# The routing stage of a two-layer kernel: one VectorE operation for the gated sum, variances by fours, tiles of coefficients on three engines, another order of TensorE's work

## What is computed

```python
# after the first layer: x (8, 128, 512), z = (x - mean) * rsqrt(var + eps) along the features
# gate: per batch and feature, one of two values, chosen by a 0/1 choice `top` of each token
x3 = x + coef * z                      # coef = top * dA + other, two numbers per batch and feature
# routed experts, on the normalised x3
xn = (x3 - mean(x3)) * rsqrt(var(x3) + eps)
logits = xn @ router_w.T + router_b    # 8 experts
top2 -> softmax over the two best, zero elsewhere
h = xn @ A.T                           # 8 experts x rank 16 = 128
out = x3 + (8 / R) * (h * gate) @ Bm
```

## Time and profile before

| | |
|---|---|
| median of 3 runs | 1065.99 us (1065.75 to 1067.38) |
| the profiled execution's own time | 1069.71 us |
| its span, first to last instruction | 1068.0 us |
| TensorE busy | 93% of the span |
| VectorE, ScalarE, GpSimd busy | 65%, 48%, 44% |
| mean granted TensorE clock | 0.973 of full speed |

### The profile page before, as it was taken

The page is one execution under the profiler, slowest core; times in us unless marked ns, Lnnn a source line. Parts: engine busy times, 40 slices in busy tenths (PEclk is TensorE's granted clock), DMA queues, the critical chain, the costliest instruction groups (busy, mean ns, idle before and its releaser), DMA issues.

```text
span 1068.0 us, 18238 instructions
## 1 busy us (share of the span) xinstructions
PE 996.8 (93%) x6004; PEld 843.0 (79%) x6004; DVE 697.6 (65%) x1827; ACT 512.6 (48%) x1328; POOL 467.5 (44%) x366
## 2 busy tenths in 40 slices
PE   5999999999999999999999999999999999869376
PEld 4888888888888888888888888888888888734263
DVE  5567565666577767677564575566567557678755
ACT  4454444444444445445543544445355354345561
POOL 4555444444444555443354344346435334226241
PEclk9999999999999999999999999999999999969768
DMA  6422222223333332333322222213222221000002
GB/s 219 161 92 87 95 95 89 91 95 96 96 97 98 98 97 83 104 112 98 106 84 84 85 67 72 83 42 98 73 74 84 80 69 53 23 21 1 0 2 79
DMA packets 50412, 87.71 MB, mean 82 GB/s; under 512 B 6368, under 2 KB 15200, under 8 KB 50336
## 3 DMA queue, kind: packets, MB, share of 16 engines
q1 hardware_dynamic: 50336, 86.76, 25.4%
HBM read 84.64 MB, written 2.10 MB: 81 GB/s over the span
## 4 chain that ended last, share of the span: by engine, by line
PE 79%; DVE 7%; issue 6%; POOL 3%; DVEq 2%; ACT 2%; DMA 1%; SPq 0%; POOLq 0%; ACTq 0%
PE pX L1731 15%; PE pX L1733 14%; PE pX L1732 14%; PE pT L1983 5%; PE oacc L1731 5%; PE oacc L1732 5%; PE oacc L1733 5%; PE pS L1915 5%; PE pS L1736 2%; PE pA L2043 1%; POOL wv_lo L570 1%; PE pX L1848 1%; PE pX L1904 1%; PE pT L1904 1%; PE pX L1736 1%
## 5 line engine op out<-in xcount | busy, mean ns | idle before, releaser
L570 POOL TENSOR_TENSOR wq_lo<-raw_q,wq_hi 128x512 fp32r<-128x512 f32 x64 | 82.6, 1290 | 264.2 <-DVE prob L1376 257.9
L1731 PE MATMUL pX<-wv_lo,cT_hi 128*128 128x256 f32 x512 | 149.5, 292 | 0.2 <-ACT q_sb L740 0.2
L1359 DVE TENSOR_TENSOR score<-pS,b_mask 128x512 f32<-128x512 f32 x64 | 44.2, 691 | 156.8 <-PE pS L1915 144.7
L868 ACT ACTIVATE prob<-score,neg_max 128x128 f32<-128x128 f32 x256 | 99.8, 391 | 97.4 <-DVE neg_max L1362 97.4
L1732 PE MATMUL pX<-wv_hi,cT_lo 128*128 128x256 f32 x512 | 144.3, 282 | 0.0
L1733 PE MATMUL pX<-wv_hi,cT_hi 128*128 128x256 f32 x512 | 144.2, 282 | 0.0
L570 POOL TENSOR_TENSOR wv_lo<-raw_v,wv_hi 128x1024 fp32r<-128x1024 f32 x32 | 77.1, 2409 | 121.9 <-ACT wv_hi L740 121.9
L740 ACT ACTIVATE v_sb<-pX 128x512 f32<-128x512 f32 x64 | 38.2, 597 | 163.6 <-PE pX L1733 163.6
L1731 PE MATMUL pX<-xT_lo,wq_hi 128*128 128x512 f32 x252 | 104.4, 414 | 5.7 <-POOL wq_lo L570 5.0
L1731 PE MATMUL oacc<-wo_lo,aT_hi 128*128 128x512 f32 x256 | 101.8, 398 | 3.5 <-DVE aT_lo L1351 2.3
L1731 PE MATMUL pX<-cT_lo,wk_hi 128*128 128x512 f32 x252 | 103.0, 409 | 0.0
(11 more groups left out here) (308 smaller groups left out, 2377.4 us busy)
## 6 DMA issues: line engine op xcount, KB each, us to landing
raw_k<-in_wk SPq DMA_DIRECT2D x64, 256.0 KB, 2.8
raw_q<-in_wq SPq DMA_DIRECT2D x64, 256.0 KB, 3.5
raw_v<-in_wv SPq DMA_DIRECT2D x32, 512.0 KB, 3.9
raw_o<-in_wo SPq DMA_DIRECT2D x64, 256.0 KB, 2.6
b_raw<-in_bias SPq DMA_DIRECT2D x64, 64.0 KB, 2.5
g_raw<-in_w_gate SPq DMA_DIRECT2D x16, 172.0 KB
g_raw<-in_w_up SPq DMA_DIRECT2D x16, 172.0 KB
f_raw<-in_w_down SPq DMA_DIRECT2D x4, 688.0 KB, 4.1
```

The lines of the kernel that those rows point to most:

```text
L570: g.tensor_tensor(w_lo[c][:], w_raw[c][:], w_hi[c][:].bitcast(F32), ALU.subtract).then_inc(s_w_lo[c], 1)
L868: e = a.activation(prob[:, b, :], score[:, b, :], ACT.Exp, bias=neg_max[:, b:b + 1], accum_out=row_sum[:, b:b + 1])
L1359: v.tensor_tensor(score[:], pS[:].rearrange("p (b s) -> p b s", b=HB), b_mask[:], ALU.add).then_inc(s_scored, 1)
L1731: mm(dst, lh, rl, start=start, stop=False, skip_group_check=lint)
```

## The change

In `gated`, VectorE now adds sigma = 1/rstd of z (two reciprocals, ahead of the stage) to the bank and multiplies by z, straight into `xr`: coef z + x = (coef + sigma) z + mean. The mean is left out of `xr` until the last step; GpSimd's addition and the tile `zc` fall away here. The statistics are one `bn_stats` for each batch, with the rest for four batches together and one power for four. `rh` is copied without a scale; the scale enters the logits (one operation for each batch) and, with 8/R, the gates. The four coefficient tiles of a batch go two to ScalarE, one to VectorE, one to GpSimd (batch 0: one and three to ScalarE and VectorE). The table load stands behind ScalarE's first five tiles. TensorE's order is routed_transposes(t + 1), router(t), coef_transposes(t + 3), and the experts' products all come after the last router. The results of batches 0 to 3 go through SBUF: ScalarE adds the mean (`lora_out`), then VectorE adds batches 0 and 1 and GpSimd 2 and 3 to `xr`, all after VectorE's second `weighed`. SP waits accordingly. The diff, without declarations, the VectorE helpers that only move and the old lists already told in words:

```diff
             for t in range(B):
-                sp.wait_ge(s_x4_done, t + 1)
+                if t in (2, 3):
+                    sp.wait_ge(s_x4_pool, t - 1)
+                else:
+                    sp.wait_ge(s_x4_done, t + 1 if t < 2 else t - 1)
                 sp.dma_start(out[t], xr[:, t, :]).then_inc(s_out[t % 2], 16)
...
-            for t in range(B):
-                pool.wait_ge(s_zc, t + 1)
-                g.tensor_tensor(xr[:, t, :], zc[:, t % 2, :], xr[:, t, :], ALU.add).then_inc(s_x3, 1)
-                if t >= 1:
-                    routed_rstd(t - 1)
-            routed_rstd(B - 1)
+            def one_coef(t):
+                g.tensor_scalar(coef[:, t, KT - 1, :], top[:, t // HB, KT - 1, t % HB, :], dA[:, KT - 1, t:t + 1],
+                                other[:, KT - 1, t:t + 1], ALU.mult, ALU.add).then_inc(s_coef_pool, 1)
+
+            def routed_rstd(i):
+                pool.wait_ge(s_x3_var, i + 1)
+                g.tensor_tensor(rs3[:, i * HB:(i + 1) * HB], ve3[:, i * HB:(i + 1) * HB], neg_half[:, 0:HB],
+                                ALU.pow).then_inc(s_x3_rstd, 1)
+
+            pool.wait_ge(s_coef_dve, 1)
+            one_coef(1)
+            one_coef(2)
+            for t in range(3, B):
+                pool.wait_ge(s_x3, t - 2)
+                one_coef(t)
+            routed_rstd(0)
+            routed_rstd(1)
+            for t in (2, 3):
+                pool.wait_ge(s_lora_sb, t + 1)
+                pool.wait_ge(s_x4_done, 2)
+                g.tensor_tensor(xr[:, t, :], lora_sb[t], xr[:, t, :], ALU.add).then_inc(s_x4_pool, 1)
...
             def routed_heads(t):
                 act.wait_ge(s_r_proj, t + 1)
-                act.wait_ge(s_x3_rstd, t + 1)
-                a.activation(rh[:, t, :], pA[:, 0:E + ER], ACT.Copy,
-                             scale=rs3[:, t:t + 1]).then_inc(s_rh, 1)
+                copy(rh[:, t, :], pA[:, 0:E + ER]).then_inc(s_rh, 1)
...
+            def lora_out(t):
+                act.wait_ge(s_l_proj, t + 1)
+                a.activation(lora_sb[t], l_bank[t % 2], ACT.Identity, bias=e_zmv[:, t, 0:1]).then_inc(s_lora_sb, 1)
+
+            weights_of(0, (3,))
+            weights_of(1, (0, 1))
+            weights_of(2, (0, 1))
+            a.activation(exp_again[:], ident[:, 0:1], ACT.Exp)
+            routed_out(0)
+            weights_of(3, (0, 1))
+            for t in range(HB):
+                routed_out(t + 1)
+                routed_heads(t)
+                weights_of(t + 4, (0, 1))
+            routed_out(5)
+            routed_heads(4)
+            routed_out(6)
+            routed_heads(5)
+            route_exp(0)
+            routed_out(7)
+            routed_heads(6)
+            routed_heads(7)
+            lora_in(0)
+            lora_in(1)
+            lora_out(0)
+            lora_in(2)
+            lora_out(1)
+            lora_in(3)
+            route_exp(1)
+            lora_out(2)
+            lora_out(3)
             for t in range(HB, B):
-                lora_out(t)
+                lora_in(t)
...
             def gated(t):
                 dve.wait_ge(s_c_trans, t + 1)
-                if t >= 2:
-                    dve.wait_ge(s_x3, t - 1)
-                v.tensor_tensor(zc[:, t % 2, :], c_bank[t % 2][:], z[:, t, :], ALU.mult).then_inc(s_zc, 1)
+                v.scalar_tensor_tensor(out=xr[:, t, :], in0=c_bank[t % 2][:], scalar=sigma[:, t:t + 1],
+                                       in1=z[:, t, :], op0=ALU.add, op1=ALU.mult).then_inc(s_x3, 1)
...
+            weights_of(0, (0, 1, 2))
+            weights_of(1, (2,))
+            weights_of(2, (2,))
             dve.wait_ge(s_e_z_again, HB)
             dve.wait_ge(s_z_act, 2)
             gated(0)
             gated(1)
+            for t in range(HB + 1):
+                if t + 3 < B:
+                    weights_of(t + 3, (2,))
+                dve.drain()
+                routed_stats(t)
+                if t == HB - 1:
+                    variances_of(0)
+                if t + 2 < 7:
+                    gated(t + 2)
+            routed_stats(5)
+            top_logits(0)
+            gated(7)
+            routed_stats(6)
+            chosen(0)
+            routed_stats(7)
+            variances_of(1)
+            gates(0)
+            for t in range(HB):
+                weighed(t)
+            top_logits(1)
+            chosen(1)
+            gates(1)
+            for t in range(HB, B):
+                weighed(t)
+            lora_sum(0)
+            lora_sum(1)
             for t in range(HB, B):
                 finished(t)
...
             def lora(t):
                 pe.wait_ge(s_hwT, t + 1)
-                if t >= 2:
-                    pe.wait_ge(s_x4_done, t - 1)
+                if 2 <= t < HB + 2:
+                    pe.wait_ge(s_lora_sb, t - 1)
+                elif t >= HB + 2:
+                    pe.wait_ge(s_x4_done, t - HB + 1)
...
             coef_transposes(0)
             coef_transposes(1)
+            routed_transposes(0)
+            coef_transposes(2)
+            for t in range(B - 1):
+                routed_transposes(t + 1)
+                if t == 0:
+                    pe.wait_ge(s_ra, 1)
+                router(t)
+                if t + 3 < B:
+                    coef_transposes(t + 3)
+            router(B - 1)
+            hidden_transpose(0)
             for t in range(HB):
+                lora(t)
+                hidden_transpose(t + 1)
             hidden_transpose(5)
             for t in range(HB, B):
                 lora(t)
                 if t + 2 < B:
                     hidden_transpose(t + 2)
```

More of the change, by code:

```diff
@@ L245, in layers_kernel @@
         post.close()
+        lora_sb = [t[:, i].rearrange("p k s -> p (k s)") for t in (e_split, e_junk) for i in range(2)]
         sum_junk = zc[:].rearrange("p i (k s) -> p i k s", k=KT)
@@ L298, in layers_kernel @@
         s_coef = sem("coef")
-        s_coef_first = sem("coef_first")
+        s_coef_dve = sem("coef_by_dve")
+        s_coef_pool = sem("coef_by_pool")
+        s_lora_sb = sem("lora_sb")
         s_const_in = sem("const_in")
@@ L1049, in _, with weights_of @@
             last.then_inc(s_sig, 1)
-            a.activation(exp_again[:], ident[:, 0:1], ACT.Exp)
             act.wait_ge(s_dA, 1)
-            def weights_of(t):
-                for lt in range(KT):
+            def weights_of(t, parts):
+                for lt in parts:
                     last = a.activation(coef[:, t, lt, :], top[:, t // HB, lt, t % HB, :], ACT.Identity,
@@ L1075, in route_exp, with lora_in @@
                              ACT.Exp).then_inc(s_r_exp, 1)
-            def lora_out(t):
+            def lora_in(t):
                 act.wait_ge(s_hw_t, t + 1)
@@ L1637, in _, with weights_of @@
             dve.drain()
-            for lt in range(KT):
-                last = v.tensor_scalar(coef[:, 0, lt, :], top[:, 0, lt, 0, :], dA[:, lt, 0:1], other[:, lt, 0:1],
-                                       ALU.mult, ALU.add)
-            last.then_inc(s_coef_first, 1)
-            dve.wait_ge(s_e_z_again, HB)
-            dve.wait_ge(s_z_act, 2)
+            def weights_of(t, parts):
+                for lt in parts:
+                    last = v.tensor_scalar(coef[:, t, lt, :], top[:, t // HB, lt, t % HB, :], dA[:, lt, t:t + 1],
+                                           other[:, lt, t:t + 1], ALU.mult, ALU.add)
+                last.then_inc(s_coef_dve, 1)
@@ L1652, in routed_stats, with variances_of @@
             def routed_stats(t):
-                dve.wait_ge(s_x3, t + 1)
                 v.bn_stats(st3[:, t, :], xr[:, t, :])
+            def variances_of(i):
                 dve.drain()
-                v.bn_aggr(mv3[:, t, :], st3[:, t, :])
+                for t in range(i * HB, (i + 1) * HB):
+                    v.bn_aggr(mv3[:, t, :], st3[:, t, :])
                 dve.drain()
-                v.tensor_scalar(ve3[:, t:t + 1], mv3[:, t, 1:2], EPS, None, ALU.add).then_inc(s_x3_var, 1)
@@ L1661, in route, with top_logits @@
-            def route(i):
-                group = slice(i * HB, (i + 1) * HB)
+                v.tensor_scalar(ve3[:, group(i)], mv3[:, group(i), 1], EPS, None, ALU.add).then_inc(s_x3_var, 1)
+            def top_logits(i):
                 dve.wait_ge(s_rh, (i + 1) * HB)
-                v.tensor_tensor(prb[:, group, 0:E], rh[:, group, 0:E], rb[:].to_broadcast([P, HB, E]), ALU.add)
+                dve.wait_ge(s_x3_rstd, i + 1)
+                for t in range(i * HB, (i + 1) * HB):
+                    v.scalar_tensor_tensor(out=prb[:, t, 0:E], in0=rh[:, t, 0:E], scalar=rs3[:, t:t + 1],
+                                           in1=rb[:, 0, :], op0=ALU.mult, op1=ALU.add)
@@ L1692, in weighed, with lora_sum @@
                                 wexp[:, t, :, :].to_broadcast([P, E, R]), ALU.mult).then_inc(s_hw, 1)
+            def lora_sum(t):
+                dve.wait_ge(s_lora_sb, t + 1)
```

(19 more changed lines are left out.)

93 lines of the change are left out of this document (26 added, 67 removed).

## The result

The changed kernel took 1060.83 us (median of 5 runs, 1060.54 to 1061.39) where the one before took 1066.98 in its 5 runs of the comparison (1065.75 to 1067.5): a ratio of 0.9946, 95% interval 0.9931 to 0.9961. Measured again beside the experiments it took 1060.63 against 1067.71, a ratio of 0.9935 (0.9922 to 0.9948). So 6.2 us and 7.1 us, faster by about 0.6%, where 7.7 was forecast; 1060.8 lies inside the range of 1056.0 to 1062.0, but 2.5 above the number and outside the forecast's own range of 1056.5 to 1060.0. Of the 2.5, 1.0 is the base: the forecast started from 1065.99, and the kernel before took 1066.98 here.

The account below looks back on a forecast made before the run. It took TensorE to bound the whole kernel, but ScalarE and then handovers the last 48 us. The stage's end came 7.9 us earlier, less 0.2 for semaphores: -7.7 from 1065.99 gives 1058.3, range 1056.0 to 1062.0 (own range 1056.5 to 1060.0).

Parts of the forecast that it names:

- Head: Stage start to x3 transposes: fused operation without GpSimd's addition and earlier first transposes let TensorE turn x3 1.7 us earlier.
- Loop: Up to the last router: TensorE becomes the bound at 1.82 us a batch; last heads copy at 1042.7, 9.3 us earlier.
- both holes: TensorE waits in the loop: 1.0 us for gated(7) behind top_logits(0), 0.9 between routers 6 and 7.
- To the second weighed: Last heads copy to batch 4's hw: four expert steps and the queued exponential make 7.2 us; hw 7.4 earlier than before.
- the lost clock: Rival, 0.20: full clock late at 1032.3 (1059.9 us), or lost in the expert steps, costing 3.7 us (1062.0 us).
- To the last addition: From hw of batch 4, products at full clock: 5.7 us instead of 8.1, last addition 9.8 us earlier.
- Outputs: Kernel end: five transfers queue behind GpSimd's additions, giving some saving back; end at 1060.1, 7.9 us earlier.
- the rival by which the outputs decide: Rival, 0.10: GpSimd additions at 1.90 (+1.3) and transfers 1.0 apart (+1.5) give 1061.1 us.
- its -6.6: The predicted sum if GpSimd's additions at the outputs cost 1.90 us each instead of 1.27.
- the clock at half after 1032: Sign of a wrong forecast: TensorE still or again at half clock after 1032 us.
- The rival by which the coefficients would not get cheaper: Rival, 0.05: GpSimd's coefficient tile costs over 2.0 us and bounds the loop; at 3.0, 1066.2 us, no change.
- the slower one: Rival, 0.05: TensorE stays at 1.2 GHz with all routers in a row and experts behind, 1072.2 us.

Follow-up runs that it names:

- the old order in the loop: Changed kernel with TensorE's loop order back to routed_transposes(t), coef_transposes(t + 2), router(t), experts still behind the last router: 1062.53 us.
- The filler: Changed kernel plus 20 unused identity transposes on TensorE, eight behind the last router, three behind each of the next four expert transposes: 1059.78 us.
- the addition: Changed kernel with the fused operation undone: VectorE multiplies into zc, GpSimd adds to xr: 1062.83 us.
- the variances: Changed kernel with the variance and its power done batch by batch again, one GpSimd power for each: 1063.0 us.
- the tiles: Changed kernel with all coefficient tiles back on ScalarE (batch 0 on VectorE), none on GpSimd: 1060.95 us, again 1060.61 us.
- the whole old order: Changed kernel with expert products of batches 0 to 3 back between the routers and the three engines' old lists: 1065.44 us.

## Why the prediction was right, and where it was off

The direction, the place and most of the steps were right; the step behind the last router was not. By its own steps:

1. **Head**, forecast -1.7: measured -1.5 (4.62 to 3.14). The table load cost nothing. The fused operation was taken at 0.69 from a form with a constant scalar; with a pointer it takes 0.75.
2. **Loop**, forecast -9.3: measured -11.1 in one trace, -9.7 in the other. The interval of the routers was right (1.80 for 1.82), and both holes were there (0.91 and 0.64 for 1.0 and 0.9). The clock was taken to rise 6.2 us after TensorE began to work, from the one rise of the earlier trace rows. In one trace it rose 6.1 us after, and the last heads copy came at 20.53, for 20.9 forecast; in the other it rose 3.1 us after, and this alone brought the copy 1.4 forward. The split was off: 4.7 of the 9.3 were put on the experts between the routers and VectorE's `route`, but the old order in the loop alone moves the copy by 4.6, and the experts between the routers by only 2.8 on top of it. "GpSimd's tile 0.5" was right (0.45 to 0.48).
3. **To the second weighed**, forecast 7.2 from heads copy to `hw`: measured 9.8. This is the step that failed. It assumed the full clock; the clock was lost, since TensorE idled before the first product. The filler puts 1.4 of the 2.6 on that (8.4 with it). Another 0.5 are the first gates: the first transpose came 1.1 after the heads copy (1040.36), not 0.6, since the loop ended earlier and VectorE's list did not. The five operations of the gates took 1.60 (1047.46 to 1049.06), not 1.3; and the steps were 1.6 apart at the full clock (1.52 forecast), which the 0.2 less behind the last of them nearly makes good. The last 0.3 is a slip of addition: 0.6 + 3 x 1.52 + 0.8 + 0.2 is 6.2, which gives 1048.9 and not 1048.6, so the terms as they stand make 7.5 and not 7.2. I had the lost clock as a rival, at 3.7 for the whole of it, and put it at small odds by a busy share over 15 us. Such a mean hides how the work is spread: TensorE now had a pause of 1.1 us behind the last router and then single short transposes, 0.57 us of work in 2 us.
4. **To the last addition**, forecast 5.7: measured 5.97.
5. **Outputs**, forecast 4.5 for the tail: measured 4.07; 0.91 share and 341 GB/s, and GpSimd's additions 1.26 each, as the sum took them. With that the rival by which the outputs decide is out. (With 1.90 the sum would have been -6.4; its -6.6 leaves out the 0.2 of the three semaphores.)

So the sum over the stage, -7.7, was measured as -7.2 and -5.8 in the two traces, and as -6.2 and -7.1 in the times. The -7.2 is luck in part: there the clock came 3 us early, which gave 1.4, and the clock lost later took as much. The -5.8 has the clock where the forecast had it, and shows what the third step missed. A sign that the prediction had named as one of being wrong, the clock at half after 1032, did show (1041.4 to 1044.8), so part of its rival of a lost clock came true: a loss of 1.4, not of 3.7. By the savings, 6.2 and 7.1 lie nearer to the forecast's 7.7 than to that rival's 4.0. The rival by which the coefficients would not get cheaper was refuted; the slower one too (the clock came earlier than before).

The experiments say +2.1 for the addition, +2.4 for the variances, 0 for the tiles and +4.7 for the whole old order (which contains the +1.8 of the loop's), 9 in all for a change worth 6 to 7: they overlap, since each only counts while the engine it relieves is the one that is late. Why the tiles' share ends at nothing in the times, beyond the 0.9 in the trace, stays open.

## What to carry to other kernels

In a tail of handovers the order of the lists is worth more than cheaper operations: here the cheaper operations in the old order gave at most 0.2% in the times. Look for an instruction that stands in an engine's queue behind work it does not need (the exponential behind four copies: VectorE waited 4.5 us for it, and moving it was worth 1.3 in the times and 2.35 in the stage), and for outputs that a new order pushes to the end, where each adds its whole transfer. After moving work out of a gap, ask what TensorE does in the gap: 20 useless transposes kept the clock and gave back more than they took, 1.5 us of the stage in the trace (0.9 in the times, which don't resolve it).

## What was not expected of the hardware

- The same kernel, at the same place, got the full clock 4.2 us or 7.2 us after the end of `dA`, 3.1 or 6.1 us after TensorE had begun to work; in six of the nine traces with all experts behind the last router and no filler the clock then fell again ahead of or in the experts' products, and came back 3.4 us later in the trace of the changed kernel above, some 6.8 later in that of the variances and in the first of the tiles.
- A VectorE multiply of 4 elements a partition took 0.75 us instead of 0.16, and one of 32 took 1.17 instead of 0.19, beside a GpSimd addition of two tiles of 128 x 512.
- The part ahead of the stage, the same in all kernels but for two reciprocals that lie in a wait, ended anywhere from 1018.5 to 1022.3 us. A single pair of profiles with 8.9 us between their spans stood for 6 to 7 us of change.
